# A local-attention stack: the scores' products moved behind the output projection, and VectorE's additions reordered with them

## The chip, the cores and the metric

The kernel runs on 1 core of one Trainium2 chip. The metric is the device time of one execution in microseconds. Three runs of the kernel before took 3993.65, 4002.0 and 4001.08 us, so the median is 4001.08 us.

## What is computed

The input is x, 8 batches of 512 tokens of 128 dimensions. One causal attention layer with 16 heads comes first, behind a modulated layer norm. Then follow six layers, each of a local attention and a feed-forward network. The local stack is what the change touches. In short, for each of the six layers:

```python
def attn_layer(x, Wqkv, qs, ksc, Wo):
    qkv = x @ Wqkv
    q, k, v = jnp.split(qkv, 3, -1)
...
    q = l2norm(q) * qs
    k = l2norm(k) * ksc
...
    q = q * cos * scale + rotate_half(q) * sin * scale
    k = k * cos * inv + rotate_half(k) * sin * inv
    out = local_attention(q, k, v)
    out = out.transpose(0, 2, 1, 3).reshape(b, n, INNER)
    return out @ Wo
...
    sim = jnp.einsum('bhwie,bhwje->bhwij', bq, bk2) * QK_SCALE
    sim = jnp.where(mask, -jnp.finfo(sim.dtype).max, sim)
    attn = jax.nn.softmax(sim, -1)
    out = jnp.einsum('bhwij,bhwje->bhwie', attn, bv2)
...
for i in range(DEPTH):
    x = attn_layer(shift_tokens(x), Wqkv[i], q_scale[i], k_scale[i], Wo[i]) + x
    x = ffn_layer(shift_tokens(x), ln_g[i], ln_b[i], W1[i], b1[i], W2[i], b2[i]) + x
```

There are 16 heads of 64. `local_attention` looks at windows of 32 tokens, each of which sees itself and the one before. `ffn_layer` is a layer norm, a product with W1, a gate with gelu and a product with W2.

Everything is in float32.

## The kernel before, in words

`adaln_block` (L1607 on) calls three stages: `modulated_attention`, `local_stack` and `last_residual`. Only `local_stack` is changed. It goes through 48 units, each one batch in one layer, and each unit has 4 tiles of 128 tokens (`t` is 0 to 3). All tiles of all units form one pipeline. While PE makes q, k and v of a tile, it works on the scores of the tile before (`back` is 1), on the probabilities and the local output of the tile two back, and on the output projection of the tile three back. `unit(u)` on each engine writes this pipeline out, and `loop` repeats it.

The order on PE is a list that is written by hand, `jobs_of(t)` (L277 to L287). Its entries, in order, are these:

- `q`, `k`, `v`: the products with the weights (L455), six matmuls each.
- `tq`, `tk`: transposes of the rotated and normalised q and k (L472).
- `ot`: transposes of the local output of the tile three back (L505). It goes into PSUM banks 0 and 1.
- `sim`: the scores of the tile one back (L485), into banks 6 and 7.
- `pt`: transposes of the probabilities of the tile two back (L477), into banks 2 and 3. PE waits there for `exp_ready` and for the bank.
- `feed`: one piece of the feed-forward network: `m1`, the mean (L509), for t = 3; `m2`, the variance (L514), for t = 0; `y`, the second product (L530), for t = 2; all in bank 1.
- `z`: the output projection of the tile three back (L465), into bank 0. It waits for `taken["ot"]`.
- `o`: the local output of the tile two back (L497).
- `h`: for t = 1 alone, the three pairs of products of the first feed-forward matrix (L522), into banks 0 and 1, then 6 and 7, then 2 and 3.

`slot_free` makes PE wait, ahead of each job, until the last users of its banks have been read. It follows the same list.

ScalarE (ACT) goes through a tile in this order: the squares of q (L571, L573), the copy of `tq` (L597), the squares of k (L575), two copies of `tk` into `k_bd` (L608), the copy of v (L618), the exponential of the tile two back (L622), the copy of `ot` (L632), the reciprocal norms (L583, L585), and the copy of `pt` (L640). Then follow the pieces of the feed-forward network.

VectorE (DVE) goes through a tile in this order: sums of squares and rotary products of q and k (L710 to L728), mask addition of the scores (L749) and maximum (L753), sum and reciprocal of the exponentials (L757, L760), for t = 3 the subtraction of the mean (L766), for t = 2 the addition of `y` to x (L773), the addition of `z` to x (L784), the division of the local output (L792), and for t = 1 the gated products (L802). GpSimd (POOL) adds the rotary parts (L826), refines the norms, normalises q and k (L846) and at the end of a tile subtracts the maximum from the scores (L874), which ACT takes up in the next tile. SyncE (SP) spreads v into the block layout by DMAs.

Of the kernel before, what the change touches and what calls it, by code (L numbers as in the profile page):

```python
# [7 lines left out]
ALU = mybir.AluOpType  # L8
ACT = mybir.ActivationFunctionType
AX = mybir.AxisListType  # L10
# [3 lines left out]
P = 128  # L14

BATCH, N, DIM = 8, 512, 128
TILES = N // P
# [5 lines left out]
DEPTH, HEADS, DH, WIN = 6, 16, 64, 32  # L23
# [117 lines left out]
def local_stack(nc, w, LAYERS, const_sb, xT, x_done, w_split, tables):  # L141
# [12 lines left out]
    ident, ones_mean, mask, rn_shift, three, ln_eps = (  # L154
        const_sb[k] for k in ("ident", "ones_mean", "mask", "rn_shift", "three", "ln_eps"))

    def alive(u, d):
        return not isinstance(u, int) or 0 <= u + d < NU

    def tiles_done(u, d, t):  # L160

        return u * TILES + (TILES * d + t + 1)
# [5 lines left out]
    def batch_of(u, d):  # L168
        return (u + d) % BATCH if isinstance(u, int) else (u + (d % BATCH)) % BATCH
# [15 lines left out]
    def columns_of(b, first, width, rows=slice(0, P)):  # L185

        if isinstance(b, int):
            return xT[rows, b * XW + first:b * XW + first + width]
        return xT[rows, bass.ds(b * XW + first, width)]
# [20 lines left out]
    with ExitStack() as ctx:  # L210
        def sb(name, shape, dtype=F32):
            return ctx.enter_context(nc.sbuf_tensor("st_" + name, shape, dtype))

        def sem(name):
            return ctx.enter_context(nc.semaphore("st_" + name))
# [21 lines left out]
        s = sb("s", [P, 2, INNER])  # L237
        mx = sb("mx", [P, 2, HEADS])
        den = sb("den", [P, 2, 2, HEADS])
        probT = sb("probT", [P, INNER])  # L240
        o = sb("o", [P, INNER])
# [19 lines left out]
        ready = {k: sem(k + "_ready") for k in KINDS}  # L261
# [3 lines left out]
        taken = {k: sem(k + "_taken") for k in KINDS if k not in ("q", "k")}  # L265
# [5 lines left out]
        max_ready, shifted, exp_ready, den_ready = sem("max_ready"), sem("shifted"), sem("exp_ready"), sem("den_ready")  # L271
# [6 lines left out]
        def jobs_of(t):  # L278
            def tile(kind, back, *banks):
                d, tt = divmod(t - back, TILES)  # L280
                return (kind, d, tt), banks

            feed = {3: [(("m1", -1, 0), (1,))], 0: [(("m2", -2, 0), (1,))], 1: [], 2: [(("y", -2, 0), (1,))]}[t]
            hidden = [(("h", -2, j), H_BANKS[j]) for j in range(HC)] if t == 1 else []
            return [tile("q", 0, 0, 1), tile("tq", 1, 2, 3), tile("k", 0, 4, 5), tile("tk", 1, 6, 7),
                    tile("v", 0, 2, 3), tile("ot", 3, 0, 1), tile("sim", 1, 6, 7), tile("pt", 2, 2, 3), *feed,
                    tile("z", 3, 0), tile("o", 2, 4, 5), *hidden]  # L287

        JOBS = [job for t in range(TILES) for job, _ in jobs_of(t)]
        BANKS = [banks for t in range(TILES) for _, banks in jobs_of(t)]  # L290
        STARTS = [sum(len(jobs_of(i)) for i in range(t)) for t in range(TILES)]
        FIRST_BANK = {job: banks[0] for job, banks in zip(JOBS, BANKS)}

        def slot_of(kind, d, index):

            first = FIRST_BANK[(kind, d, index)] * BANK
            return ps[:, first:min(first + INNER, NBANKS * BANK)]
# [32 lines left out]
        with nc.Block() as block:  # L330
# [346 lines left out]
            def _(dve):  # L677
# [4 lines left out]
                def remainder_half(u, d, half):  # L682

                    dve.wait_ge(xs_high, halves_done(u, d, half))
                    cols = slice(half * 2 * P, (half + 1) * 2 * P)
                    dve.tensor_tensor(xs[:, 1, cols], columns_of(batch_of(u, d), half * 2 * P, 2 * P),
                                      xs[:, 0, cols].bitcast(F32), ALU.subtract).then_inc(xs_ready, 1)
# [7 lines left out]
                def unit(u):  # L695
                    start = isinstance(u, int)
                    for t in range(TILES):
                        n = tiles_done(u, 0, t)
# [38 lines left out]
                            remainder_half(u, 1, 0)  # L737
                        if t == 0 and alive(u, 0) and alive(u, -1):
                            remainder_half(u, 0, 1)
                        d1, t1 = divmod(t - 1, TILES)  # L740
                        if alive(u, d1):


                            par = t1 % 2
                            dve.wait_ge(ready["sim"], n - 1)
                            if not (start and n < 4):
                                dve.wait_ge(ready["pt"], n - 3)
                            scores = s[:, par, :].rearrange("p (h k) -> p h k", h=HEADS)
                            dve.tensor_tensor(scores, slot_of("sim", d1, t1).rearrange("p (h k) -> p h k", h=HEADS),  # L749
                                              mask[0 if t1 == 0 else 1].unsqueeze(1).to_broadcast([P, HEADS, 2 * WIN]),  # L750
                                              ALU.add).then_inc(taken["sim"], 1)
                            dve.wait_ge(taken["sim"], n - 1)
                            dve.tensor_reduce(mx[:, par, :], scores, AX.X, ALU.max).then_inc(max_ready, 1)  # L753
                        if alive(u, d2):

                            dve.wait_ge(exp_ready, n - 2)
# [22 lines left out]
                        if alive(u, d3):  # L779

                            dve.wait_ge(ready["z"], n - 3)
                            for rows, first in ((LOW, 0), (HIGH, 1)):
                                x = columns_of(batch_of(u, d3), t3 * P + first, P, rows)
                                last = dve.tensor_tensor(x, slot_of("z", d3, t3)[rows, 0:P], x, ALU.add)  # L784
                            last.then_inc(taken["z"], 1)
                        if alive(u, d2):

                            dve.wait_ge(ready["o"], n)
                            dve.wait_ge(den_ready, 2 * (n - 2))
                            if not (start and n < 4):  # L790
                                dve.wait_ge(ready["ot"], n - 3)
                            dve.tensor_tensor(  # L792
                                o[:, :].rearrange("p (h d) -> p h d", h=HEADS),
                                slot_of("o", d2, t2).rearrange("p (h d) -> p h d", h=HEADS),
                                den[:, t2 % 2, 1, :].unsqueeze(2).to_broadcast([P, HEADS, DH]),
                                ALU.mult).then_inc(taken["o"], 1)
                        if t == 1 and alive(u, -2):
                            for j in range(HC):
# [5 lines left out]
                                                         ALU.add, ALU.mult).then_inc(taken["h"], 1)  # L804

                loop(dve, unit, ST_FILL.get('dve', 0))

            @block.gpsimd
# [864 lines left out]
```

## Time and profile before

| what | value |
|---|---|
| median of 3 runs | 4001.08 us (3993.65 to 4002.0) |
| the profiled execution's own time | 4002.27 us |
| its span, first to last instruction | 4000.5 us |
| mean granted clock of TensorE | 0.985 of full speed |
| PE busy | 3733.8 us (93%) |
| DVE busy | 3151.4 us (79%) |
| POOL busy | 2781.7 us (70%) |
| ACT busy | 2570.7 us (64%) |

The shares are over the whole span. A view by stretches (rows 1, 8 and the second of rows 9 below) gives the stretch as start and end in us, its length, the busy time of each engine with the number of instructions, the granted clock, the share of the DMA engines and GB/s. The first 750 us or so are the first attention stage, in which PE works with gaps. The local stack fills nearly all of the rest. A timeline's row gives the start of a group in us, its length in us, the engine, the line, the operation, what it writes and reads, the shape and the count. A bracket holds the idle time of the engine ahead of the group and what ended it. Ends of matmuls are modelled, so that groups of PE can overlap by some 0.1 us.

### The profile page before, as it was taken

The page shows a single profiled execution, that of the slowest core. Times are in us where ns is not written, and L with a number is a line of the kernel's source. Part 1 is how long each engine was busy: PE and PEld are TensorE (multiplying, and loading weights), DVE is VectorE, ACT ScalarE, POOL GpSimd, SP SyncE. Part 2 cuts the span into 40 slices and gives each one's busy share as a digit, 9 for nine tenths or more (in the row PEclk, how much of TensorE's full clock was granted, in tenths as well). Part 3 has the DMA queues.
Part 4 walks back from the last instruction along what each step waited for, and adds up shares of the span by engine and source line. Part 5 has one row for each costly group of instructions (what it writes and reads, how often), then busy time and mean ns, then how long its engine had stood idle before and what let it go on. Part 6 is the DMA issues. An engine that isn't in the chain of part 4 may idle for free. (4 is left out here: it accounts for less than half of the span.)

```text
span 4000.5 us, 109740 instructions
## 1 busy us (share of the span) xinstructions
PE 3733.8 (93%) x42284; PEld 2927.6 (73%) x42284; DVE 3151.4 (79%) x4328; ACT 2570.7 (64%) x3589; POOL 2781.7 (70%) x2249
## 2 busy tenths in 40 slices
PE   6998897799999999999999999999999999999996
PEld 4766675677777777777777777777777777777774
DVE  4666664888888888888888888888888888888884
ACT  3555554566666666666666666666666767676763
POOL 2554552777777777777777777777777777777772
PEclk9999998999999999999999999999999999999998
DMA  1122110322223222232222232222322223222222
GB/s 42 59 74 73 66 68 13 100 66 60 62 63 100 66 58 64 55 103 63 68 53 66 82 79 64 61 61 62 102 66 62 60 60 99 62 70 54 68 54 62
DMA packets 157178, 267.01 MB, mean 67 GB/s; under 512 B 32062, under 2 KB 51644, under 8 KB 152380
## 3 DMA queue, kind: packets, MB, share of 16 engines
q1 hardware_dynamic: 157116, 266.19, 24.7%
q8 instruction: 38, 0.62, 0.1%
q14 instruction: 24, 0.20, 0.0%
HBM read 44.81 MB, written 26.21 MB: 18 GB/s over the span
## 5 line engine op out<-in xcount | busy, mean ns | idle before, releaser
L826 POOL TENSOR_TENSOR st_qk_rot<-st_qk_rot,st_qk_sq 128x1024 f32<-128x1024 f32 x384 | 920.5, 2402 | 692.7 <-DVE st_qk_sq L728 692.7
L455 PE MATMUL st_ps<-st_wqkv,st_xs 128*128 128x512 f32 x3456 | 949.6, 410 | 25.8 <-issue 18.3
L455 PEld LDWEIGHTS st_ps<-st_wqkv,st_xs 128*128 128x128 f32 x3456 | 608.2, 189 | 194.6 <-issue 75.2
L846 POOL TENSOR_TENSOR st_qk_rot<-st_qk_rot,st_rn 128x1024 f32<-128x1024 f32 x384 | 723.1, 1904 | 15.0
L710 DVE TENSOR_REDUCE st_nt<-st_qk_sq 128x16 f32<-128x1024 f32 x384 | 466.2, 1214 | 234.6 <-ACT st_qk_sq L573 233.2
L728 DVE TENSOR_TENSOR st_qk_sq<-st_ps,st_rot 128x512 f32<-128x512 f32 x768 | 490.1, 678 | 0.0
L714 DVE TENSOR_TENSOR st_qk_rot<-st_ps,st_rot 128x1024 f32<-128x1024 f32 x384 | 466.1, 1214 | 9.8 <-PE st_ps L472 9.8
L472 PE MATMUL st_ps<-consts_sb,st_qk_rot 128*128 128x128 f32 x3072 | 402.2, 274 | 27.9 <-DVE st_hid L802 14.9
L571 ACT ACTIVATE st_qk_sq<-st_ps 128x512 f32<-128x512 f32 x192 | 115.0, 599 | 486.3 <-PE st_ps L455 485.8
L472 PEld LDWEIGHTS st_ps<-consts_sb,st_qk_rot 128*128 128x128 f32 x3072 | 355.8, 141 | 94.1 <-DVE st_hid L802 34.7
L465 PEld LDWEIGHTS st_ps<-st_oT,st_wo 128*128 128x128 f32 x3072 | 368.8, 192 | 69.5 <-issue 67.7
L1458 DVE TENSOR_REDUCE at_nmx<-at_s 128x1 f32<-128x512 f32 (+3 forms) x512 | 236.9, 486 | 209.3 <-PE at_s L1103 208.5
L608 ACT ACTIVATE st_k_bd<-st_ps 64x1024 f32<-64x1024 f32 x384 | 389.5, 1014 | 3.1 <-PE st_ps L472 0.8
L485 PE MATMUL st_ps<-st_k_bd,st_qT 128*32 128x128 f32 x12288 | 375.2, 274 | 3.0 <-ACT st_k_bd L608 3.0
L465 PE MATMUL st_ps<-st_oT,st_wo 128*128 128x128 f32 x3072 | 376.2, 276 | 0.5 <-ACT st_oT L632 0.3
L497 PE MATMUL st_ps<-st_v_bd,st_probT 128*32 128x128 f32 x12288 | 375.2, 274 | 1.3 <-ACT st_probT L640 1.3
L874 POOL TENSOR_TENSOR st_s<-st_s,st_mx 128x1024 f32<-128x1024 f32 x192 | 366.0, 1906 | 6.1 <-DVE st_mx L753 6.1
L1279 ACT ACTIVATE at_probT<-at_t 128x512 f32<-128x512 f32 (+1 forms) x384 | 201.3, 526 | 255.8 <-PE at_t L1122 248.1
L485 PEld LDWEIGHTS st_ps<-st_k_bd,st_qT 128*32 128x32 f32 x12288 | 326.4, 110 | 35.6 <-ACT st_k_bd L608 20.5
L497 PEld LDWEIGHTS st_ps<-st_v_bd,st_probT 128*32 128x32 f32 x12288 | 323.7, 110 | 24.5 <-issue 1.5
L522 PE MATMUL st_ps<-st_xc,st_w 128*128 128x512 f32 (+1 forms) x576 | 261.8, 604 | 52.6 <-DVE xT_sb L784 43.2
L1542 POOL TENSOR_TENSOR at_qs<-at_q,consts_sb 128x512 fp32r<-128x512 f32 x128 | 135.3, 1074 | 216.8 <-DVE at_q L1409 200.0
(144 smaller groups left out, 6944.8 us busy)
## 6 DMA issues: line engine op xcount, KB each, us to landing
st_v_bd<-st_v_tok SPq DMA_DIRECT2D x1152, 128.0 KB, 2.4
st_v_bd<-st_v_tok SPq DMA_DIRECT2D x672, 64.0 KB, 2.1
wqkv_parts<-at_w_parts SPq DMA_DIRECT2D x18, 1024.0 KB, 4.6
st_wqkv<-wqkv_parts SPq DMA_DIRECT2D x18, 1024.0 KB, 7.0
at_w_raw<-in_wqkv SPq DMA_DIRECT2D x18, 512.0 KB, 5.1
rotary_tables<-at_rot SPq DMA_DIRECT2D x6, 512.0 KB, 3.4
st_rot<-rotary_tables SPq DMA_DIRECT2D x24, 128.0 KB, 2.4
st_wo<-in_wo SPq DMA_DIRECT2D x6, 512.0 KB, 4.4
```

The source lines that it names most:

```text
L455: last = pe.matmul(out[:, c * 512:(c + 1) * 512], xs[:, x_part, t * P:(t + 1) * P], rhs, start=(n == 0), stop=(n == len(PASSES) - 1))
L465: last = pe.matmul(out[:, 0:P], wo[:, c, :], oT[:, c * P:(c + 1) * P], start=(c == 0), stop=(c == IC - 1))
L472: last = pe.transpose(out[:, c * P:(c + 1) * P], src[:, c * P:(c + 1) * P], ident)
L485: last = pe.matmul(out[g * WIN:(g + 1) * WIN, c * P:(c + 1) * P], qT[:, par, c * P + g * WIN:c * P + (g + 1) * WIN], k_bd[:, c, :, key:key ...
L497: last = pe.matmul(out[g * WIN:(g + 1) * WIN, c * P:(c + 1) * P], probT[:, c * P + g * WIN:c * P + (g + 1) * WIN], v_bd[:, par, g, :, c * ...
L608: last = act.activation(k_bd[rows, :, a, WIN + t1 * P:WIN + (t1 + 1) * P], src[rows, :, :], ACT.Copy)
L710: dve.tensor_reduce(nt[:, 2 + par, heads], qk_sq[:, cols].rearrange("p (h d) -> p h d", d=DH), AX.X, ALU.add).then_inc(ss_sum, 1)
L714: dve.tensor_tensor(qk_rot[:, cols].rearrange("p (h d) -> p h d", d=DH), slot_of("qk"[a], 0, t).rearrange("p (h d) -> p h d", d=DH), rot[: ...
L728: last = dve.tensor_tensor(dst[:, :, g, :], src[:, :, 1 - g, :], sines.unsqueeze(1).to_broadcast([P, HEADS, DH // 2]), ALU.mult)
L826: pool.tensor_tensor(qk_rot[:, cols], qk_rot[:, cols], qk_sq[:, cols], ALU.add).then_inc(rot_done[a], 1)
L846: pool.tensor_tensor(view, view, rn[:, par, heads_of(a)].unsqueeze(2).to_broadcast([P, HEADS, DH]), ALU.mult).then_inc(normed[a], 1)
L874: pool.tensor_tensor(scores, scores, mx[:, tt % 2, :].unsqueeze(2).to_broadcast([P, HEADS, 2 * WIN]), ALU.subtract).then_inc(shifted, 1)
```

## The change

In `jobs_of` the entry `sim` moves from its place between `ot` and `pt` to one between `z` and `o`. On DVE the mask addition and the maximum move from ahead of the sum of the exponentials to behind the addition of `z`. The order between the other blocks stays as it is, and nothing is added or removed. ACT, POOL and SP have the same instructions in the same order.

```diff
             return [tile("q", 0, 0, 1), tile("tq", 1, 2, 3), tile("k", 0, 4, 5), tile("tk", 1, 6, 7),
-                    tile("v", 0, 2, 3), tile("ot", 3, 0, 1), tile("sim", 1, 6, 7), tile("pt", 2, 2, 3), *feed,
-                    tile("z", 3, 0), tile("o", 2, 4, 5), *hidden]
+                    tile("v", 0, 2, 3), tile("ot", 3, 0, 1), tile("pt", 2, 2, 3), *feed,
+                    tile("z", 3, 0), tile("sim", 1, 6, 7), tile("o", 2, 4, 5), *hidden]
```

On DVE these lines of `unit` stand ahead of the blocks for the sum of the exponentials, `m1`, `y` and `z` before, and directly behind them, ahead of the block for `o`, now:

```python
d1, t1 = divmod(t - 1, TILES)
if alive(u, d1):
    par = t1 % 2
    dve.wait_ge(ready["sim"], n - 1)
    if not (start and n < 4):
        dve.wait_ge(ready["pt"], n - 3)
    scores = s[:, par, :].rearrange("p (h k) -> p h k", h=HEADS)
    dve.tensor_tensor(scores, slot_of("sim", d1, t1).rearrange("p (h k) -> p h k", h=HEADS),
                      mask[0 if t1 == 0 else 1].unsqueeze(1).to_broadcast([P, HEADS, 2 * WIN]),
                      ALU.add).then_inc(taken["sim"], 1)
    dve.wait_ge(taken["sim"], n - 1)
    dve.tensor_reduce(mx[:, par, :], scores, AX.X, ALU.max).then_inc(max_ready, 1)
```

On PE, a tile with t = 1 stands like this in the program before, from the products of v to the first feed-forward products. L505 are the transposes `ot`, L485 the scores, L477 the transposes `pt`, L465 is `z`, L497 `o` and L522 `h`:

```order
L455 MATMUL st_ps<-st_wqkv,st_xs 128x512 x6
L314 REGISTER_ALU
L505 MATMUL st_ps<-consts_sb,st_o 128x128 x8
L485 MATMUL st_ps<-st_k_bd,st_qT 32x128 x32
L477 MATMUL st_ps<-consts_sb,st_s 128x128 x8
L465 MATMUL st_ps<-st_oT,st_wo 128x128 x8
L494 REGISTER_ALU
L497 MATMUL st_ps<-st_v_bd,st_probT 32x128 x32
L520 ISA
L522 MATMUL st_ps<-st_xc,st_w 128x512 x4
```

The same place in the changed program:

```order
L455 MATMUL st_ps<-st_wqkv,st_xs 128x512 x6
L314 REGISTER_ALU
L505 MATMUL st_ps<-consts_sb,st_o 128x128 x8
L477 MATMUL st_ps<-consts_sb,st_s 128x128 x8
L465 MATMUL st_ps<-st_oT,st_wo 128x128 x8
L485 MATMUL st_ps<-st_k_bd,st_qT 32x128 x32
L494 REGISTER_ALU
L497 MATMUL st_ps<-st_v_bd,st_probT 32x128 x32
L520 ISA
L522 MATMUL st_ps<-st_xc,st_w 128x512 x4
```

The 32 products of the scores have left the place between `ot` and `pt`, so that `pt` follows `ot` at once. They now stand between `z` and `o`. It is the same in all four tiles of a unit, with the piece of `feed` between `pt` and `z`.

On DVE, this is the piece of the difference for a tile without a piece of the feed-forward network. L749 and L753 are mask addition and maximum before (L781 and L785 now), L757 and L760 sum and reciprocal (L743 and L746 now), L784 the addition of `z` (L770 now):

```order
-L749 TENSOR_TENSOR st_s<-st_ps,consts_sb 128x1024
-L753 TENSOR_REDUCE st_mx<-st_s 128x16
-L757 TENSOR_REDUCE st_den<-st_s 128x16
-L760 RECIPROCAL st_den<-st_den 128x16
-L784 TENSOR_TENSOR xT_sb<-st_ps,xT_sb 64x128 x2
+L743 TENSOR_REDUCE st_den<-st_s 128x16
+L746 RECIPROCAL st_den<-st_den 128x16
+L770 TENSOR_TENSOR xT_sb<-st_ps,xT_sb 64x128 x2
+L781 TENSOR_TENSOR st_s<-st_ps,consts_sb 128x1024
+L785 TENSOR_REDUCE st_mx<-st_s 128x16
 L792 TENSOR_TENSOR st_o<-st_ps,st_den 128x1024
```

Mask addition and maximum have gone behind the addition of `z`, and only the division of `o` still follows them.

## Rows read from the trace of the kernel before

**Rows 1.** Busy us (count) of PE, PEld, DVE, ACT, POOL; clock, DMA share, GB/s

```profile
800.00:3900.00 3100.00, 3008.52 (x36880) 2381.29 (x36878) 2609.21 (x3324) 2114.51 (x2769) 2370.51 (x1895) 1.00 0.27 68
```

**Rows 2.** Timeline, PE, a tile with t = 3, whole

```profile
2017.34 1.66 PE L455 MATMUL st_ps<-st_wqkv,st_xs 128*128 128x512 f32 x6
...
2019.63 1.64 PE L455 MATMUL st_ps<-st_wqkv,st_xs 128*128 128x512 f32 x6
...
2023.37 1.04 PE L505 MATMUL st_ps<-consts_sb,st_o 128*128 128x128 f32 x8
...
2024.36 1.95 PE L485 MATMUL st_ps<-st_k_bd,st_qT 128*32 128x128 f32 x64
...
2026.40 1.06 PE L477 MATMUL st_ps<-consts_sb,st_s 128*128 128x128 f32 x8
...
2028.33 1.95 PE L465 MATMUL st_ps<-st_oT,st_wo 128*128 128x128 f32 x16
...
2030.20 1.95 PE L497 MATMUL st_ps<-st_v_bd,st_probT 128*32 128x128 f32 x64
...
2032.21 1.66 PE L455 MATMUL st_ps<-st_wqkv,st_xs 128*128 128x512 f32 x6
```

**Rows 3.** Timeline, ACT, the same tile, up to the exponential

```profile
2021.30 1.02 ACT L575 ACTIVATE st_qk_sq<-st_ps 128x1024 f32<-128x1024 f32 x1 [0.36 <-PE st_ps L455]
...
2022.22 2.04 ACT L608 ACTIVATE st_k_bd<-st_ps 64x1024 f32<-64x1024 f32 x2
...
2024.29 1.02 ACT L618 ACTIVATE st_v_tok<-st_ps 128x1024 f32<-128x1024 f32 x1
...
2025.21 1.05 ACT L622 ACTIVATE st_s<-st_s 128x1024 f32<-128x1024 f32 x1
```

**Rows 4.** Timeline, `ot` and exponential in tiles with t = 0 and t = 1

```profile
1971.26 1.06 PE L505 MATMUL st_ps<-consts_sb,st_o 128*128 128x128 f32 x8
...
1972.90 1.05 ACT L622 ACTIVATE st_s<-st_s 128x1024 f32<-128x1024 f32 x1
...
1985.98 1.04 PE L505 MATMUL st_ps<-consts_sb,st_o 128*128 128x128 f32 x8
...
1987.83 1.05 ACT L622 ACTIVATE st_s<-st_s 128x1024 f32<-128x1024 f32 x1
```

**Rows 5.** Timeline, the tile with t = 2

```profile
2007.06 1.06 PE L505 MATMUL st_ps<-consts_sb,st_o 128*128 128x128 f32 x8 [0.37 <-issue]
...
2008.37 1.05 ACT L622 ACTIVATE st_s<-st_s 128x1024 f32<-128x1024 f32 x1
...
2009.62 1.01 ACT L632 ACTIVATE st_oT<-st_ps 128x1024 f32<-128x1024 f32 x1
...
2010.87 2.74 PE L530 MATMUL st_ps<-st_hid,st_w 128*128 128x512 f32 x6
```

**Rows 6.** Who waited for whom, PE: us in total, times, longest

```profile
PE st_ps L522 <- DVE xT_sb L784: 43.2, 46, 1.0
```

**Rows 7.** Waits of PE in the first attention stage: the first and last of nine

```profile
177.32 0.70 PE L1170 MATMUL at_m<-at_hT,at_wqk 128*128 128x512 f32 x1 [1.51 <-DVE at_q L1409]
...
646.98 0.47 PE L1097 MATMUL at_s<-at_k,at_qs 128*128 128x512 f32 x1 [1.40 <-DVE at_nmx L1458]
```

**Rows 8.** Busy time and granted clock around one such wait (257.5 to 259.0)

```profile
257.40:259.06 1.66, 0.17 (x2) 0.09 (x1) 1.66 (x4) 1.21 (x2) 1.58 (x2) 1.00 0.00 0
259.06:262.47 3.41, 3.41 (x8) 2.23 (x9) 1.55 (x4) 0.68 (x2) 3.33 (x4) 0.50 0.00 0
```

**Rows 9.** Timeline, the stack's last `y` product, and the clock over it

```profile
3941.75 4.54 PE L530 MATMUL st_ps<-st_hid,st_w 128*128 128x512 f32 x6 [2.24 <-ACT st_oT L632]
```
```profile
3942.05:3945.40 3.35, 3.35 (x5) 1.33 (x4) 0.00 (x0) 0.00 (x0) 0.00 (x0) 0.50 0.00 0
```

**Rows 10.** Timeline, DVE, the t = 3 tile: maximum and division of `o`

```profile
2028.07 1.22 DVE L753 TENSOR_REDUCE st_mx<-st_s 128x16 f32<-128x1024 f32 x1
...
2032.22 1.23 DVE L792 TENSOR_TENSOR st_o<-st_ps,st_den 128x1024 f32<-128x1024 f32 x1 [0.40 <-PE st_ps L497]
```

More of the change, by code:

```diff
@@ L739, in unit @@
                             remainder_half(u, 0, 1)
[L740 to L753, printed above, removed]
                         if alive(u, d2):
@@ L785, in unit @@
                             last.then_inc(taken["z"], 1)
+                        d1, t1 = divmod(t - 1, TILES)
+                        if alive(u, d1):
+                            par = t1 % 2
+                            dve.wait_ge(ready["sim"], n - 1)
+                            if not (start and n < 4):
+                                dve.wait_ge(ready["pt"], n - 3)
+                            scores = s[:, par, :].rearrange("p (h k) -> p h k", h=HEADS)
+                            dve.tensor_tensor(scores, slot_of("sim", d1, t1).rearrange("p (h k) -> p h k", h=HEADS),
+                                              mask[0 if t1 == 0 else 1].unsqueeze(1).to_broadcast([P, HEADS, 2 * WIN]),
+                                              ALU.add).then_inc(taken["sim"], 1)
+                            dve.wait_ge(taken["sim"], n - 1)
+                            dve.tensor_reduce(mx[:, par, :], scores, AX.X, ALU.max).then_inc(max_ready, 1)
                         if alive(u, d2):
```

## The prediction

> **What bounds the kernel now.** I read the busy time by engine in the steady part of the stack first, because the page's shares mix it with the other stages. From 800 to 3900 us PE is busy in 3008.5 of 3100 us, at a granted clock of 1.00 [rows 1]. That is 97%. The next engine, DVE, has 84%. So whatever PE waits for in the stack is paid almost in full, and the question is which waits of PE the new order makes and which it takes away.
>
> Then the timeline of one tile, the one with t = 3. PE goes from `ot` (start 2023.37) to the scores (2024.36), to `pt` (2026.40), over `m1` to `z` (2028.33), to `o` (2030.20) and to the next q (2032.21), with hardly a gap [rows 2]. A PE that never waits does not show how close it is to waiting. For that I looked at what `pt` needs, which is the exponential on ACT. ACT runs a chain without a pause there. It starts with the squares of k, which wait for the product of k. Then come two copies into `k_bd`, the copy of v and the exponential, which ends at 2025.21 + 1.05 = 2026.26 [rows 3]. `pt` starts 0.14 us behind that [rows 2]. So the scores' products are not just work that stands in front of `pt`. They fill, almost to the tenth of a microsecond, the time in which `pt` could not run anyway. The other tiles are like it. `ot` ends at 1972.32 and the exponential at 1973.95 for t = 0, at 1987.02 and 1988.88 for t = 1 [rows 4], and at 2008.12 and 2009.42 for t = 2 [rows 5].
>
> One wait is in the way of the feed-forward products for t = 1: PE stood 43.2 us in 46 waits of some 0.94 us ahead of L522, for DVE's addition of `z` (L784) [rows 6]. DVE did that addition late, because mask, maximum, sum and reciprocal stood ahead of it.
>
> **The change, part by part.**
>
> *Scores out of the gap.* `pt` now follows `ot`, but nothing that the exponential waits for has become earlier. ACT's order is as before, and its chain begins with the product of k, ahead of anything that moved. So PE waits from the end of `ot` to the end of the exponential plus 0.14 us. That is 2026.26 + 0.14 - 2024.41 = 1.99 us for t = 3 [rows 2, 3]. By the same sum it is 1.77 for t = 0, 2.00 for t = 1 [rows 4] and 1.44 for t = 2 [rows 5]. From `pt` on the old times hold, relative to the product of k.
>
> *Scores behind `z`.* Their 1.95 us [rows 2] are now added in front of `o`. In the tiles with t = 0, 1 and 3 `pt` had been bound by the exponential within 0.05 us, so that the tile grows by all of it. For t = 2, `y` needs the copy of `ot`, which ends at 2010.63, and it started at 2010.87 [rows 5]; there some 0.1 us may be won. Over 192 tiles: 192 x 1.95 = 374 us. I take off 5 us for t = 2 and 5 us for the first and last units, where PE waits for other things.
>
> *DVE's order.* The addition of `z` now comes as soon as `z` is there, two jobs ahead of L522. The 43 us [rows 6] go. What is late next there? `h` in banks 6 and 7 needs the mask addition, which runs during `o` and the first pair of products, and `o` alone covers it, with 1.95 us [rows 2] for 1.2 us of work [rows 10]. I price it at nothing.
>
> *Maximum later.* The scores end at about the old end of `o`, less 0.1. DVE then does mask addition, maximum and the division of `o`, at 1.2 us each [rows 10], some 3.7 us. `o` has ended 1.9 us in, and the next tile's product of k, which needs the bank that the division frees, starts 2.29 us behind the product of q [rows 2], 4.2 us in. The slack is 0.5 us, so I count nothing. GpSimd's subtraction of the maximum is the last thing of its tile, and what waits for it is the exponential of the next tile, which stands behind the products of q, k and v there [rows 2, 3]; those cover it.
>
> The sum without the clock: 4002.3 + 374 - 10 - 43 = 4323 us. The profiled execution (4002.27) is 1.2 us above the median of the runs, which changes nothing.
>
> *The clock.* The stack before never has PE idle for more than 1 us in its steady part, and its clock stays at 1.00, full speed, 2.4 GHz [rows 1, 6]. Now it has 188 or so waits of 1.4 to 2.0 us. For such waits I looked in the first attention stage. Between 60 and 650 us PE has nine waits of 1.4 to 1.8 us [rows 7]. Behind or within seven of them the clock goes to 0.50 (1.2 GHz), mostly for 3.41 us, as behind the one that ended at 259.0 [rows 8]; behind two of them, the one that ended at 177.32 and a like one at 493.66, it stayed. In the stack's drain there is one more, a wait of 2.24 us for the copy of `ot`. Half speed follows at 3942.05, and the six matmuls of `y` take 4.54 us in place of 2.74 [rows 5, 9], 1.80 us more. Against this stands that PE works more densely around the waits in the stack than in the attention, and that the 46 waits of 0.94 us never brought it down. I take the share of the attention stage, 7 of 9, for the three longer waits of a unit (3 x 48 x 7/9 = 112), and one in six for the wait of 1.44 us (8), between 0 of 46 and 7 of 9 and nearer to the first for the denser work. Each of the 120 falls costs half of 3.41 us, 1.7 us, which agrees with the 1.80. That is 204 us. The bounds are 0, if none falls, and 192 x 1.80 = 346 us, if all do.
>
> The Trainium skill has two rules on this that disagree here. TensorE: Matmul & The Clock Gate, the section on HAM oscillation, asks only that PE have no idle gap longer than any wait that I expect here; by that rule there are no falls, and the time is 4323 us. Its section on a second failure mode tells of a kernel in which short idles between groups of matmuls were enough for the clock to oscillate; by that one falls are to be expected. This trace agrees with the second [rows 8, 9].
>
> So the forecast is 4323 + 204 = 4527, rounded to **4525 us**.
>
> **The rivals.**
>
> *The waits come, but the clock holds.* For it: the clock stayed at 1.00 behind two of the nine waits, and the stack is denser. Against it: the seven others, and the one of the stack itself [rows 8, 9]. Time 4323 us. The first of the two rules of the Trainium skill leads here.
>
> *DVE becomes late as well.* The division of `o` now stands behind two more operations, with 0.5 us to spare before the product of k. If DVE comes to the mask addition late by one of its operations, 1.2 us [rows 10], the 0.5 us are used up and each tile loses 0.7 us. That is 192 x 0.7 = 134 us more, and the time is some 4660 us. Against it: DVE has nothing else to do at that point, since it waits for the scores.
>
> *Faster.* The exponential is not what `pt` waits for in the new order, because ACT gets its chain done by the end of `ot`. Then PE has no new wait, the scores only change places, and the waits ahead of L522 go: 4002 - 43 = 3959 us. The point from which it decides is an exponential that ends 1.3 to 1.85 us earlier [rows 2 to 5]. Against it: four operations of 5.1 us follow the product of k on ACT back to back, and no edit touches one of them.
>
> *No change.* Some slack that I do not see takes up the new waits, so that PE was not the bound. Rows 1 leave 3% for that. The change could also not do what it says, but the order of the built program shows the scores moved in all four tiles.
>
> **How the numbers follow.** Forecast with falls: 0.70, and its own range, from 80 to 160 falls, is 4459 to 4595. Clock holds: 0.17. DVE late as well: 0.06. Faster: 0.04. No change: 0.03. The range of 8 in 10 takes in the forecast's own range and the rival at 4323, from 4315 to 4595 us. The measurement can tell about 0.2% from no change. Faster by more than that has 0.04, within it 0.03, slower 0.70 + 0.17 + 0.06 = 0.93.
>
> **What would show it.** Right, step by step: a wait of PE or its weight loads ahead of L477 in every tile, 1.4 to 2.0 us, released by ACT's L622; the wait ahead of L522 gone; tiles that are 1.95 us longer at full clock; a granted clock that falls to 0.50 for 3.4 us again and again in the stack, with a mean near 0.945 over it (1 - 0.5 x 120 x 3.41 / 3740). Wrong: `pt` starts at the end of `ot` (then ACT's chain was read wrongly); the clock stays at 1.00 (then the time is near 4323); the product of k waits for the division of `o`.

## The result and the profile after

The changed kernel takes 4382.2 us (median of 4 runs, 4378.5 to 4383.95), the kernel before 4000.73 us, now the median of four executions. The ratio is 1.0956, with a 95% interval from 1.0937 to 1.0975. The experiments' ratios are to the kernel before as it was timed beside each of them, at 3996.91 to 3999.59 us. One of six executions of an experiment below (VectorE's new order for t = 1 and 2) was in a slow state, 6964.53 us at a mean clock of 0.862 where the five others took 3961.81 to 3970.89 us, and its ratio leaves it out. The profiled execution has a span of 4382.1 us where it was 4000.5 us, 381.6 us more.

The page of the changed kernel, part 1, and the slices of PE and its clock:

```profile
PE 3826.8 (87%) x42284; PEld 3028.0 (69%) x42284; DVE 3157.8 (72%) x4328; ACT 2574.5 (59%) x3589; POOL 2782.3 (63%) x2249
...
PE   6988895888889888889888898888898888889886
...
PEclk9999998999999999999999999999999999999997
```

Each engine has as many instructions as before. Only PE is busy for much longer, by 93 us, since some of its work runs at half speed, and all shares fall. The slices of the clock hide what happens in the stack, since a tenth is too coarse. The view by stretches shows it, for the stretch of [rows 1]:

```profile
800.00:3900.00 3100.00, 2767.25 (x33019) 2212.97 (x33012) 2339.34 (x2973) 1893.51 (x2475) 2119.34 (x1693) 0.97 0.24 62
```

PE is busy in 2767 of 3100 us where it was 3008, and the granted clock is 0.97 where it was 1.00. Who PE waits for, from 800 to 4250 us:

```profile
PE st_ps L477 <- ACT st_s L622: 331.4, 184, 2.0
...
PE st_ps L505 <- issue: 17.1, 45, 0.4
PE st_ps L472 <- DVE st_hid L802: 14.8, 45, 0.3
```

One wait is new, that of `pt` for the exponential, and it is in every tile. The wait of L522 for the addition of `z` [rows 6] is gone. The new one in tiles with t = 0, 1 and 2, of which the first is longer than 1.06 us because the clock falls in it:

```profile
1972.17 1.67 PE L477 MATMUL st_ps<-consts_sb,st_s 128*128 128x128 f32 x8 [1.77 <-ACT st_s L622]
...
1990.17 1.06 PE L477 MATMUL st_ps<-consts_sb,st_s 128*128 128x128 f32 x8 [1.99 <-ACT st_s L622]
...
2011.45 1.06 PE L477 MATMUL st_ps<-consts_sb,st_s 128*128 128x128 f32 x8 [1.43 <-ACT st_s L622]
```

Here is a tile with t = 3 at full clock, which answers to [rows 2], from `ot` to the next q:

```profile
2102.85 1.04 PE L505 MATMUL st_ps<-consts_sb,st_o 128*128 128x128 f32 x8
2105.88 1.06 PE L477 MATMUL st_ps<-consts_sb,st_s 128*128 128x128 f32 x8 [2.00 <-ACT st_s L622]
2106.85 1.12 PE L509 MATMUL st_ps<-xT_sb,consts_sb 128*128 x2
2107.81 1.95 PE L465 MATMUL st_ps<-st_oT,st_wo 128*128 128x128 f32 x16
2109.68 1.95 PE L485 MATMUL st_ps<-st_k_bd,st_qT 128*32 128x128 f32 x64
2111.45 1.93 PE L497 MATMUL st_ps<-st_v_bd,st_probT 128*32 128x128 f32 x64
2113.39 1.65 PE L455 MATMUL st_ps<-st_wqkv,st_xs 128*128 128x512 f32 x6
```

From `ot` to `pt` it is 3.03 us, exactly as before (2026.40 - 2023.37) [rows 2]. The scores' products had filled that time, and now nothing does. From the scores to `o` it is 1.77 us, less than the 1.95 that the row gives as their length. And this is a tile with t = 3 in which the clock falls, with the view by stretches for the stretch behind its wait:

```profile
2029.83 1.32 PE L477 MATMUL st_ps<-consts_sb,st_s 128*128 128x128 f32 x8 [1.99 <-ACT st_s L622]
...
2030.94 1.93 PE L509 MATMUL st_ps<-xT_sb,consts_sb 128*128 x2
...
2032.66 2.55 PE L465 MATMUL st_ps<-st_oT,st_wo 128*128 128x128 f32 x16
```
```profile
2030.50:2033.90 3.40, 3.40 (x12) 2.32 (x11) 1.88 (x3) 1.73 (x5) 3.16 (x5) 0.50 0.03 10
```

`pt`, `m1` and `z` take 1.32, 1.93 and 2.55 us in place of 1.06, 1.12 and 1.95.

The distance from one product of q to the next sorts all this. These are means over the tiles of the steady part (44 of each t), from the starts in the timeline, in us:

| t | before | after, at full clock | after, with a stretch at half clock | tiles with one |
|---|---|---|---|---|
| 0 | 14.92 | 16.66 | 18.00 | 15 of 44 |
| 1 | 19.99 | 20.72 | 22.32 | 15 of 44 |
| 2 | 17.39 | 18.93 | none | 0 of 44 |
| 3 | 14.89 | 16.60 | 18.15 | 34 of 44 |

At full clock the four tiles together are 5.71 us longer, 48 x 5.71 = 274 us. A fall of the clock costs 1.51 us in the mean, and the stack has some 70 of them, 106 us. The sum, 380 us, is within 2 us of what the span grew by.

### The profile page after: what moved, and what is told of

It is laid out like the page before. It is cut to its first block and busy times, and to the rows that moved or that the text cites. A ratio compares the mean times of both kernels' runs of the same rounds, so it can differ in the third digit from the quotient of the medians.

```text
span 4382.1 us, 109785 instructions
## 1 busy us (share of the span) xinstructions
PE 3826.8 (87%) x42284; PEld 3028.0 (69%) x42284; DVE 3157.8 (72%) x4328; ACT 2574.5 (59%) x3589; POOL 2782.3 (63%) x2249
## 5 line engine op out<-in xcount | busy, mean ns | idle before, releaser
L826 POOL TENSOR_TENSOR st_qk_rot<-st_qk_rot,st_qk_sq 128x1024 f32<-128x1024 f32 x384 | 916.4, 2392 | 884.6 <-DVE st_qk_sq L728 884.6
L477 PE MATMUL st_ps<-consts_sb,st_s 128*128 128x128 f32 x1536 | 241.4, 309 | 346.5 <-ACT st_s L622 346.5
L465 PEld LDWEIGHTS st_ps<-st_oT,st_wo 128*128 128x128 f32 x3072 | 420.1, 213 | 97.4 <-issue 96.8
L477 PEld LDWEIGHTS st_ps<-consts_sb,st_s 128*128 128x128 f32 x1536 | 191.2, 156 | 386.4 <-issue 386.4
L465 PE MATMUL st_ps<-st_oT,st_wo 128*128 128x128 f32 x3072 | 417.0, 294 | 0.0
L781 DVE TENSOR_TENSOR st_s<-st_ps,consts_sb 128x1024 f32<-128x1024 f32 x192 | 235.3, 1225 | 221.2 <-PE st_ps L485 221.2
L485 PE MATMUL st_ps<-st_k_bd,st_qT 128*32 128x128 f32 x12288 | 376.6, 275 | 0.8 <-ACT st_k_bd L608 0.8
L497 PE MATMUL st_ps<-st_v_bd,st_probT 128*32 128x128 f32 x12288 | 370.6, 273 | 0.0
L485 PEld LDWEIGHTS st_ps<-st_k_bd,st_qT 128*32 128x32 f32 x12288 | 324.9, 110 | 24.6 <-ACT st_k_bd L608 1.2
```

The source lines that it names most:

```text
L465: last = pe.matmul(out[:, 0:P], wo[:, c, :], oT[:, c * P:(c + 1) * P], start=(c == 0), stop=(c == IC - 1))
L477: last = pe.transpose(out[:, c * P:(c + 1) * P], s[:, par, c * P:(c + 1) * P], ident)
L485: last = pe.matmul(out[g * WIN:(g + 1) * WIN, c * P:(c + 1) * P], qT[:, par, c * P + g * WIN:c * P + (g + 1) * WIN], k_bd[:, c, :, key:key ...
L497: last = pe.matmul(out[g * WIN:(g + 1) * WIN, c * P:(c + 1) * P], probT[:, c * P + g * WIN:c * P + (g + 1) * WIN], v_bd[:, par, g, :, c * ...
L826: pool.tensor_tensor(qk_rot[:, cols], qk_rot[:, cols], qk_sq[:, cols], ALU.add).then_inc(rot_done[a], 1)
```

## The experiments

### VectorE's part alone, TensorE's part alone

The first keeps the reordered DVE and puts back the old line of `jobs_of`:

```diff
-                    tile("v", 0, 2, 3), tile("ot", 3, 0, 1), tile("pt", 2, 2, 3), *feed,
-                    tile("z", 3, 0), tile("sim", 1, 6, 7), tile("o", 2, 4, 5), *hidden]
+                    tile("v", 0, 2, 3), tile("ot", 3, 0, 1), tile("sim", 1, 6, 7), tile("pt", 2, 2, 3), *feed,
+                    tile("z", 3, 0), tile("o", 2, 4, 5), *hidden]
```

> The scores' products stand at their old place between ot and pt; only VectorE's new order (addition of z ahead of mask and maximum) is kept. My theory: all of the loss is on TensorE's side, in the wait for the exponential. So no wait ahead of pt (its 333 us go), the clock stays at 1.00 in the stack, the 43 us of waits ahead of L522 stay gone, and the division of o ends 1.1 us later than before, which holds the product of k by 0.1 to 0.2 us in three tiles of four. That gives some 3977 us (3958 to 3990), faster than before. Rival: VectorE's new order is part of the loss; then this is over 4010 us, with waits of the product of k of 0.5 us and more.

Measured: 4005.39 us, ratio 1.0013 (1.0004 to 1.0022). So no more than some 6 us of the loss comes from VectorE's part alone. But the gain that I expected did not come. From its waits of PE and of the weight loads:

```profile
PE st_ps L455 <- DVE st_o L792: 19.0, 90, 0.3
```
```profile
PEld st_ps L455 <- DVE st_o L792: 51.6, 139, 0.5
```

L522 waits no more, and the tiles with t = 1 are 0.56 us shorter (19.43). Those with t = 0 and 3 are 0.25 and 0.48 us longer (15.17, 15.37), because the product of k stands until DVE has divided `o`. The product of k starts 0.23 to 0.49 us later in three tiles of four, where I had expected 0.1 to 0.2. I had that mechanism, at less than half its size.

The second is the kernel before with the new line of `jobs_of` alone, the reverse of the diff above.

> TensorE's new order with VectorE's old one. VectorE then stands at the mask addition until the scores at the end of the tile are there, and the addition of z comes some 4.4 us behind the scores. My theory: the wait ahead of pt is as in the changed kernel (1.4 to 2.0 us, it does not hang on VectorE), and a new one of 2 to 3 us comes ahead of the next product of q or of h, for z's bank. Some 4382 + 192 x 2.6 = 4880 us (4750 to 5000). Rival: VectorE's order does not matter, then the time is within 30 us of 4382.

Measured: 5479.37 us, in a single execution, so without an interval. The mechanism is there, but I had its size wrong by a factor of two and more:

```profile
PE st_ps L455 <- DVE xT_sb L784: 521.5, 138, 4.8
PE st_ps L477 <- ACT st_s L622: 337.7, 182, 2.0
PE st_ps L522 <- DVE xT_sb L784: 129.7, 45, 2.9
```

The wait ahead of `pt` is the same 2.0 us as in the changed kernel, so it does not hang on DVE. The wait of the next q for `z`'s bank is 3.8 us in the mean, where I had put 2.6. And two waits per tile brought 296 falls of the clock where the changed kernel has some 70: 1259 us at half speed, which my sum had left out. DVE's part of the change is not a gain of its own but what makes TensorE's part bearable.

### Filling the gap

The first makes the eight transposes of `ot` twice, the same values into the same place:

```diff
-                                for c in range(IC):
+                                for c in [*range(IC), *range(IC)]:
                                     last = pe.transpose(out[:, c * P:(c + 1) * P], o[:, c * P:(c + 1) * P], ident)
```

> The changed kernel with the eight transposes of ot made twice, into the same bank with the same values: 1.04 us of work in the gap ahead of pt, so that the gap of idle time is 0.4 to 0.95 us and pt starts when it did. My theory: the wait costs nothing by its filling, and what goes is the clock: no stretch at 0.50 in the stack's steady part, time 4382 - 107 = 4275 us (4260 to 4295), though TensorE does 192 us more work. Rival: the clock has nothing to do with idle gaps of this length, then the 70 stretches at half speed stay and the time is within 10 us of 4382 or above.

Measured: 4500.98 us, ratio 1.1256. By its time it refutes the theory, but the profile shows something else. Waits of PE, and the DMA queue of the instructions on the page:

```profile
PE st_ps L477 <- ACT st_s L622: 156.0, 160, 1.1
PE st_ps L455 <- issue: 137.8, 34, 4.5
```
```profile
q8 instruction: 390, 6.39, 0.6%
```

The changed kernel reads 38 packets of instructions, 0.62 MB; this one ten times that. At the turn of the loop PE stood up to 4.5 us for no engine that the profile shows, and the clock fell in or right behind those waits, at the end of tiles with t = 3 (12 times) or the start of those with t = 0 (26 times). In the tiles with t = 1 and 2 there were no falls (0 of 88), and their length was as at full clock, 20.73 and 18.92 us. To be rid of the confusion I filled the gap again with fewer instructions, one product ahead of `ot`'s transposes, which overwrite it:

```diff
                                 pe.wait_ge(taken["o"], tiles_done(u, d, index))
+                                pe.matmul(out[:, 0:4 * P].rearrange("p (a b) -> p a b", b=P), ident,
+                                          ident.unsqueeze(1).to_broadcast([P, 4, P]), start=True, stop=True)
                                 for c in range(IC):
```

> The changed kernel with one product of 512 columns ahead of the transposes of ot, into the bank that they then overwrite: 0.86 us of work, with four instructions for TensorE per tile and not sixteen as in the kernel with doubled transposes. My theory: the idle gap ahead of pt is 0.5 to 1.15 us, pt starts when it did, no stretch at half speed in the steady part, no wait of 4.5 us at the turn of the loop, which came from the longer instruction list; tiles at full clock as long as in the changed kernel: 16.65, 20.72, 18.92, 16.60 us, time 4382 - 107 = 4275 us (4260 to 4295). Rival: half speed comes whatever the gap is, then 4375 and above; or the loop turn still costs 4.5 us in most units, then 4400 to 4500.

Measured: 4267.74 us, ratio 1.0684 (1.0669 to 1.0699), 114 us less than the changed kernel by medians (109 by the two ratios), with more work. Its waits, and the stretch from 800 to 3900 us:

```profile
PE st_ps L477 <- ACT st_s L624: 153.4, 170, 1.1
```
```profile
800.00:3900.00 3100.00, 2908.62 (x34391) 2267.69 (x34393) 2409.67 (x3065) 1944.73 (x2553) 2184.08 (x1747) 1.00 0.25 63
```

The clock is 1.00 in all of it. The tiles take 16.65, 20.72, 18.92 and 16.58 us, those of the changed kernel at full clock. So the clock's share of the loss is shown: 109 to 114 us, at waits of up to 2.0 us, and none at waits of up to 1.1 us.

### ScalarE's chain

In the new order the copies of `tk` into `k_bd` are needed only behind `z`, but ACT still makes them ahead of the exponential. This kernel moves three blocks of ACT's `unit` ahead of them. The order was `k_bd`, v, exponential, `round_half` (the copy of x), `ot`. It becomes exponential, v, `ot`, `k_bd`, `round_half`:

```diff
+                        if alive(u, d2):
+                            act.wait_ge(shifted, n - 2)
+                            act.activation(s[:, t2 % 2, :], s[:, t2 % 2, :], ACT.Exp).then_inc(exp_ready, 1)
-                        if alive(u, d1):
-                            act.wait_ge(ready["tk"], n - 1)
...
                         if alive(u, 0):
                             par = t % 2
                             act.wait_ge(ready["v"], n)
...
-                        if alive(u, d2):
-                            act.wait_ge(shifted, n - 2)
-                            act.activation(s[:, t2 % 2, :], s[:, t2 % 2, :], ACT.Exp).then_inc(exp_ready, 1)
...
                             act.activation(oT[:, :], slot_of("ot", d3, t3), ACT.Copy).then_inc(taken["ot"], 1)
+                        if alive(u, d1):
+                            act.wait_ge(ready["tk"], n - 1)
...
```

> The changed kernel with ScalarE's order changed too: the exponential, the copy of v and the copy of ot ahead of the two copies into k_bd, which the scores now need only behind z. My theory: what held pt was ScalarE's chain behind the product of k. The exponential then ends some 6.1 us behind the start of the product of q instead of 8.9, pt waits 0.3 us at most (for the copy of v, its bank), no stretch at half speed is left, and a unit takes 14.9 + 15.2 + 19.0 + 17.3 = 66.4 us in place of 67.2 before. Time some 3967 us (3945 to 4000), faster than before. Rival: another wait takes its place (scores for k_bd, o for the copy of pt, or the norms), each 0.5 us and more per tile, and the time is above 4050 us.

Measured: 4086.53 us, ratio 1.0218 (1.0204 to 1.0232). The theory was right on its point. `pt` waits 35.3 us in all, now for the copy of v, and the stack's steady part has no fall. But the time is the rival's: another wait took the place, though none of the three that it names:

```profile
PE st_ps L455 <- DVE st_o L792: 80.4, 90, 1.1
PE st_ps L477 <- ACT st_v_tok L612: 35.3, 135, 0.4
```

With the gap gone, DVE has no slack. In the tiles with t = 0 and 2 it waited for ACT's copy of x, which I had put last, and the division of `o` behind it came late for the product of k in the tile that follows. L686 also took 1.57 us in place of 0.41, having started within GpSimd's operation L826, which stands first here:

```profile
1974.15 2.35 POOL L826 TENSOR_TENSOR st_qk_rot<-st_qk_rot,st_qk_sq 128x1024 f32<-128x1024 f32 x1 [1.31 <-DVE st_qk_sq L728]
...
1975.21 1.57 DVE L686 TENSOR_TENSOR st_xs<-xT_sb,st_xs 128x256 fp32r<-128x256 f32 x1 [1.14 <-ACT st_xs L550]
```

The next kernel puts that copy back ahead of the copies into `k_bd` (exponential; v; `ot`; `round_half`; `k_bd`).

> As the kernel with ScalarE's exponential early, but the copy of x for the next unit (L550) goes ahead of the copies into k_bd too. In the run before this one, VectorE waited 1.2 us for it in the tiles with t = 0 and t = 2, and then needed 1.5 us in place of 0.4 for its own part, so that the division of o was late and the next product of k waited 1 us. My theory: with the copy early, these waits go, tiles take 14.95, 19.2, 17.4 and 14.95 us, and the time is some 3970 us (3950 to 3990), 30 us faster than before. Rival: VectorE's order alone (division of o behind mask and maximum) makes the product of k late; then the waits for L792 stay over 40 us in all and the time is 4000 us or above.

Measured: 3979.05 us, ratio 0.9959 (0.9944 to 0.9973), some 0.4% faster than before and clear of the noise. L686 takes 0.41 us and waits for nobody, and the wait for L792 is no more in the list of PE:

```profile
1998.19 0.41 DVE L686 TENSOR_TENSOR st_xs<-xT_sb,st_xs 128x256 fp32r<-128x256 f32 x1
```
```profile
PE st_ps L477 <- ACT st_v_tok L612: 36.4, 139, 0.4
```

Tiles take 14.96, 19.22, 17.49 and 15.06 us. So the new order of PE is not bad in itself. It was bad in front of ACT's order.

### Where the scores stand beside o

One edit, `sim` ahead of `z` in place of behind it:

```diff
-                    tile("z", 3, 0), tile("sim", 1, 6, 7), tile("o", 2, 4, 5), *hidden]
+                    tile("sim", 1, 6, 7), tile("z", 3, 0), tile("o", 2, 4, 5), *hidden]
```

> The changed kernel with the scores between the feed piece and z, so that z stands between them and o. The wait for the exponential stays as it is. My theory: directly ahead of o, the 32-wide products of the scores overlap with those of o by 0.18 us, which is why they cost 1.77 us from start to start there and not 1.95. With z between, that is gone: 0.1 to 0.2 us more in every tile at full clock, and up to 0.2 us more for the product of k, as VectorE has mask, maximum and division behind the addition of z in a row. Time 4382 + 30 to 75 = some 4430 us (4400 to 4460). Rival: the 0.18 us is only how ends of products are modelled; then the tiles at full clock are as long as in the changed kernel but for the waits of k, 4382 to 4400.

Measured: 4440.08 us, ratio 1.1114 (1.1098 to 1.113). A tile with t = 3:

```profile
2033.89 1.95 PE L485 MATMUL st_ps<-st_k_bd,st_qT 128*32 128x128 f32 x64
2035.78 2.05 PE L465 MATMUL st_ps<-st_oT,st_wo 128*128 128x128 f32 x16
2037.76 1.96 PE L497 MATMUL st_ps<-st_v_bd,st_probT 128*32 128x128 f32 x64
```

The scores take 1.89 us to the next start, and `z` 1.98 where it took 1.87 ahead of the scores. The 1.77 us are gone, and the tile grew with them, so the shorter distance from start to start is no artefact of modelled ends. The three jobs and the way into them are 0.29 us longer (t = 1, in the mean). The product of k loses 0.2 to 0.4 us more to the late division, which is more than I had put down. That there were fewer falls (26 of 176 tiles in the profiled execution) hid some of it.

Where those falls lie says something on the clock. The waits ahead of `pt` were 2.00 us for t = 0, 1 and 3, and the clock fell in 0, 7 and 13 of 44 tiles. For t = 2 the wait was 1.43 us as in the changed kernel, where no tile had a fall, and here 6 of 44 had one. This is one of them, with the stretch behind its wait:

```profile
2241.65 1.56 PE L477 MATMUL st_ps<-consts_sb,st_s 128*128 128x128 f32 x8 [1.44 <-ACT st_s L622]
```
```profile
2242.10:2245.40 3.30, 3.30 (x9) 1.91 (x8) 2.35 (x5) 2.08 (x4) 2.59 (x2) 0.50 0.00 0
```

### A version that beats both

The waits ahead of L522, which the change took away, were all in one tile of four, the one with t = 1. These two kernels have the old order on PE, and DVE's mask addition and maximum behind the addition of `z` only for t = 1 and 2, or only for t = 1. On DVE:

```diff
-                        if alive(u, d1):
+                        if t != 1 and alive(u, d1):
...
+                        if t == 1 and alive(u, d1):
```

The second condition heads a copy of the block, ahead of the one for `o`.

> The kernel before, with VectorE's new order for t = 1 and t = 2 alone. From the run with VectorE's new order in all tiles: tiles with t = 1 and 2 were 0.56 and 0.12 us shorter, those with t = 0 and 3 were 0.25 and 0.48 us longer. My theory: the shorter ones stay and the longer ones go back, but for 0.2 us where the product of k behind t = 2 waits; 48 x 0.5 to 0.68 = 24 to 33 us less, some 3970 us (3965 to 3985). Rival: gain and loss belong together, since VectorE's later division of o is paid in the next tile; then it is within 8 us of 4000.

> The kernel before, with VectorE's new order for t = 1 alone, where the addition of z gates the feed-forward products. From the tiles of the two runs before: t = 1 takes 18.98 us in place of 19.99, and t = 0, 2 and 3 go back to 14.91, 17.39 and 14.88 us, since the 0.48 us that t = 3 lost came from the late division of o in the tile with t = 2. My theory: 48 x 1.01 = 49 us less than before, 3948 to 3955 us, and 15 us less than with t = 1 and 2. Rival: the late division in the tile with t = 1 is paid in the tile behind it; then no better than with t = 1 and 2, some 3970 us.

> The kernel with VectorE's new order for t = 1 and 2 once more, on the same chip as the one with t = 1 alone, because one of its six runs lay far off: some 3968 us, 15 us over the one with t = 1 alone.

Measured: with t = 1 and 2, 3968.53 us and, again, 3966.89 us (ratios 0.9927 and 0.9928). With t = 1 alone, 3951.71 us, ratio 0.9889 (0.9873 to 0.9904). The 15 us between them came as expected: the late division in the tile with t = 2 costs the next one 0.5 us. In the tile with t = 1 it costs nothing: the next k starts 2.83 us behind its q as before, and the feed-forward products stand between `o` and that k. `o` and `h` of the best kernel:

```profile
1969.54 1.96 PE L497 MATMUL st_ps<-st_v_bd,st_probT 128*32 128x128 f32 x64
1971.43 5.42 PE L522 MATMUL st_ps<-st_xc,st_w 128*128 128x512 f32 x12
```
```profile
800.00:3900.00 3100.00, 3042.91 (x37301) 2409.69 (x37299) 2635.84 (x3354) 2136.83 (x2794) 2384.74 (x1909) 1.00 0.27 69
```

PE is busy in 3043 of 3100 us there, and tiles with t = 1 take 18.99 us where they took 19.99.

## Why the prediction was right, and where it was off

The forecast was 4525 us with a range from 4315 to 4595, and slower at 0.93. The measured 4382 us is in the range and has the forecast sign, but it lies between the two cases, and outside the own range of the likelier one (4459 to 4595). It is in the stated range only because that was stretched down to take in the rival at 4323. By its steps:

*Scores out of the gap.* Right to a hundredth. The waits were to be 1.77, 2.00, 1.44 and 1.99 us for t = 0 to 3; they are 1.77, 2.00, 1.43 and 2.00 in the mean. The kernel with ACT's order changed shows the cause: with the exponential early, they go.

*Scores behind z, 192 x 1.95 = 374 us.* This term was too large. The length of a group of overlapping products is not what it costs. From start to start the scores take 1.77 us ahead of `o`. That is 192 x 0.18 = 35 us less. That both are 32 wide and so run into each other would explain it, and fits with the 1.89 us ahead of `z`; it is argued, not shown. At full clock the tiles with t = 0 and 3 grew by 1.74 and 1.71 us, where the prediction had 1.95. The trace had a warning: `z` is 1.95 us long as well and takes 1.87 us to the start of `o` [rows 2], so that a length was no price. I also missed that `o` hands over sooner: the next product of q no longer waits for the addition of `z` (2.01 to 1.86 us for t = 2), and `h` starts 1.04 us earlier, not 0.94.

*The waits ahead of L522.* Right, 43 us.

*Maximum later, at nothing.* Right for this change: PE has no wait for L792, and k starts 2.29 us behind q as before. But the slack of 0.5 us was as thin as it looked; in four of the other kernels it was gone, and k started 0.2 to 1.2 us later.

*The sum without the clock, 4323 us.* Measured 4000.5 + 274 = 4275 by the tiles, and 4267.74 us with the clock held by the filler. Of the 48 us, 35 are the length of the scores, and the rest is about what the earlier handing over gives.

*The clock, 120 falls at 1.7 us.* The mechanism was right and both factors were too large: some 70 falls at 1.51 us. The step that failed is the share. I took 7 of 9, from waits of the attention stage, for all three longer waits. It was 34 of 44 for t = 3, which is that share, but 15 of 44 for t = 0 and for t = 1, and 0 of 44 for the 1.43 us of t = 2. The waits for t = 1 and t = 3 have the same length, so length alone does not decide; the kernel with the scores ahead of `z` says so too, with falls behind waits of 1.43 us and none behind 44 waits of 2.00. What does decide is left open here. The nine waits were also not the whole of the attention stage's falls. There are four more between 60 and 650 us, and ahead of one of them the only wait over 0.15 us since 200 us was one of 0.91:

```profile
207.66 0.92 PE L1155 MATMUL at_m<-consts_sb,at_mx_cols 128*128 128x128 f32 x4 [0.91 <-DVE at_mx_cols L1466]
```
```profile
207.86:211.27 3.41, 3.41 (x16) 3.22 (x14) 1.87 (x4) 0.60 (x1) 0.00 (x0) 0.50 0.11 46
```

So a share of falls per wait of a given length could not be carried over from that stage. The price is below the 1.7 us, which fits with work that does not quite double at half speed: from start to start `m1` took 1.72 us for 0.96. The mean clock of the stack was to be 0.945 and is 0.96:

```profile
706.00:4273.00 3567.00, 3171.14 (x37746) 2540.18 (x37750) 2688.34 (x3412) 2169.32 (x2836) 2436.04 (x1947) 0.96 0.24 61
```

The Trainium skill, TensorE: Matmul & The Clock Gate, tells in its section on a second failure mode of short idles between groups of matmuls that make the clock oscillate. The trace of the changed kernel agrees, with some 70 falls behind waits of 1.77 to 2.00 us. Its section on HAM oscillation warns of longer gaps alone, and by it there would have been none.

*The rivals.* The clock that holds (4323 us) came nearer to the time than the forecast, 59 us off against 143, but by two errors that cancel in part, 48 us too much for the scores and 106 us of falls left out: that is luck. A chance of 0.70 for 80 falls and more rested on nine waits of another stage. It was too high, though the some 70 falls missed its bound by little. That DVE becomes late was not seen in the changed kernel, and is what held back the one with ACT's order changed.

## What to carry to other kernels

A PE that never waits may stand right at the edge of a wait. Before a job is moved away from where it stands, look at what the job behind it waits for: if that is ready only as the moved job ends, the job was filling a gap, and moving it pays its length a second time. Where an order is written out by tiles, change it in the tile that has the wait alone: here one tile in four held all the gain, and the same edit in the others gave it back.

## What the runs showed of the hardware

- In the changed kernel waits of TensorE of 1.77 to 2.00 us in work that is dense otherwise brought the granted clock to 0.50 for 3.4 us in 64 of 132 tiles, and 44 waits of 1.43 us never did. In the kernel with the scores ahead of `z`, 1.43 us did so in 6 of 44 tiles, and 2.00 us in 0, 7 and 13 of 44 for t = 0, 1 and 3. Waits of up to 1.12 us did so in none of 176 in the stack of the kernel with the filler; in the attention stage the clock fell behind one of 0.91 us.
- In the changed kernel, two groups of 64 instructions 32 wide directly behind each other take 1.77 us from start to start. The scores take 1.89 us ahead of `z`, which is 128 wide, and `z` then takes 1.98 us to the start of `o`, in place of 1.87 with transposes ahead of it and not the scores. That the width is the cause is argued from this, not shown apart. With ACT's order changed, the tiles with t = 1 have the scores right ahead of `o` too and take 1.88 us, so that width is not all of it.
- 64 more instructions on PE in a unit of the loop (798 matmuls and as many weight loads in a unit before) came with instructions being read again and again, 390 packets in place of 38, and with waits of up to 4.5 us for no engine at the turn of the loop. With 16 more there were 39 packets and no such wait.
- DVE's subtraction L686 took some 1.54 us in place of 0.41 where it started within GpSimd's operation L826, and ended 0.28 us behind that operation each time. Where it started 0.15 us ahead of L826, and ran beside it from there, it took 0.41. I did not try it apart.
